# A decoder block on one core: constant products between the chunks of maxima in latent attention, and the next norm's statistics in two parts

## The reference

```
def mla_attention(x, Wq, Wdkv, Wuk, Wuv, Wo, ln_g, ln_b):
    q = (x @ Wq.T).reshape(b, t, 16, 16).transpose(0, 2, 1, 3)
    latent = layernorm(x @ Wdkv.T, ln_g, ln_b)
    k = (latent @ Wuk.T).reshape(b, t, 16, 16).transpose(0, 2, 1, 3)
    v = (latent @ Wuv.T).reshape(b, t, 16, 16).transpose(0, 2, 1, 3)
    q, k = apply_rope(q), apply_rope(k)
    scores = jnp.einsum('bhqd,bhkd->bhqk', q, k) / np.sqrt(16)
    scores = jnp.where(causal, scores, -jnp.inf)
    attn = jax.nn.softmax(scores, axis=-1)
    out = jnp.einsum('bhqk,bhkd->bhqd', attn, v).transpose(0, 2, 1, 3).reshape(b, t, 256)
    return out @ Wo.T
```

## Time and profile before

| | |
|---|---|
| three runs | 2920.39 us median, 2918.30 to 2927.64 |
| the profiled execution | 2920.24 us |
| its span, first to last instruction | 2918.5 us |
| mean granted clock of TensorE | 0.939 |
| TensorE busy | 2728.7 us (93%) |
| VectorE busy | 1394.6 us (48%) |
| ScalarE busy | 1090.1 us (37%) |
| GpSimd busy | 298.3 us (10%) |

### The profile page before, as it was taken

The page is one execution under the profiler, slowest core; times in us unless marked ns, Lnnn a source line. Parts: engine busy times, 40 slices in busy tenths (PEclk is TensorE's granted clock), DMA queues, the critical chain, the costliest instruction groups (busy, mean ns, idle before and its releaser), DMA issues.

```text
span 2918.5 us, 43672 instructions
## 1 busy us (share of the span) xinstructions
PE 2728.7 (93%) x16662; PEld 1708.1 (59%) x16663; DVE 1394.6 (48%) x3906; ACT 1090.1 (37%) x2028; POOL 298.3 (10%) x457
## 2 busy tenths in 40 slices
PE   7999999988999999988999999998999999986998
PEld 4565665454565665454555665455556565456997
DVE  3434466643333456643333456643333457643443
ACT  3444232543444332543443332543453332531221
POOL 1000010122000010122000010122000010023111
PEclk9999996998999996998999996988999997988999
DMA  3000000001000000001000000001000000022111
GB/s 95 11 12 1 15 1 1 2 13 40 12 12 0 15 1 1 2 13 40 11 12 1 15 1 1 1 13 40 12 12 1 15 1 1 2 124 86 54 54 40
DMA packets 32426, 57.09 MB, mean 20 GB/s; under 512 B 6981, under 2 KB 23443, under 8 KB 31859
## 3 DMA queue, kind: packets, MB, share of 16 engines
q1 hardware_dynamic: 27490, 41.56, 4.5%
q0 software_dynamic: 4752, 13.02, 1.2%
HBM read 40.24 MB, written 14.32 MB: 19 GB/s over the span
## 4 chain that ended last, share of the span: by engine, by line
PE 85%; issue 4%; DVE 4%; ACT 3%; POOL 2%; another core or an unknown queue 1%; DMA 0%; DVEq 0%; ACTq 0%; POOLq 0%
PE ps L942 9%; PE ps L1189 8%; PE ps L914 8%; PE ps L1157 8%; PE ps L887 7%; PE ps L1207 6%; PE ps L872 5%; PE ps L932 5%; PE ps L1278 4%; PE ps L1292 4%; PE ps L897 4%; PE ps L1034 3%; PE ps L1052 2%; PE ps L843 1%
## 5 line engine op out<-in xcount | busy, mean ns | idle before, releaser
L1157 PE MATMUL ps<-arena 32*128 32x512 f32 (+3 forms) x1536 | 480.2, 642 | 13.6 <-DVE arena L1552 10.2
L1380 DVE TENSOR_REDUCE neg_max<-ps 128x1 f32<-128x128 f32 (+7 forms) x256 | 194.0, 758 | 608.8 <-PE ps L917 550.8
L780 ACT ACTIVATE arena<-ps 128x1024 f32<-128x1024 f32 (+1 forms) x320 | 300.5, 939 | 453.6 <-PE ps L1189 453.1
L1189 PE MATMUL ps<-arena 32*128 32x256 f32 (+1 forms) x2560 | 400.0, 424 | 0.0
L914 PE MATMUL ps<-arena 128*128 128x512 f32 (+3 forms) x768 | 303.2, 507 | 31.0 <-ACT arena L707 15.6
L942 PE MATMUL ps<-arena 128*128 128x512 f32 (+3 forms) x768 | 319.2, 503 | 5.3 <-ACT arena L698 1.4
L1189 PEld LDWEIGHTS ps<-arena 32*128 32x128 f32 x2560 | 240.2, 205 | 135.4 <-issue 106.9
L698 ACT ACTIVATE arena<-ps 128x512 f32<-128x512 f32 (+3 forms) x384 | 188.1, 491 | 295.9 <-PE ps L932 293.9
L914 PEld LDWEIGHTS ps<-arena 128*128 128x128 f32 x768 | 143.4, 197 | 168.6 <-issue 137.9
L1157 PEld LDWEIGHTS ps<-arena 32*128 32x128 f32 x1536 | 195.9, 218 | 75.3 <-DVE arena L1562 23.7
L887 PE MATMUL ps<-turned_t,arena 128*128 128x512 f32 x512 | 230.6, 604 | 1.1 <-ACT turned_t L669 1.1
(11 more groups left out here) (215 smaller groups left out, 3819.8 us busy)
## 6 DMA issues: line engine op xcount, KB each, us to landing
arena<-in_w_qkv SPq DMA_DIRECT2D x32, 384.0 KB, 3.0
arena<-in_w SPq DMA_DIRECT2D x2, 4096.0 KB, 16.9
xin<-in_x SPq DMA_DIRECT2D x5, 1024.0 KB, 5.6
xres_ids<-sorted_res SPq DMA_DIRECT2D x35, 129.0 KB, 2.2
xin<-sorted_rows SPq DMA_DIRECT2D x35, 128.0 KB
w_out<-in_w_out SPq DMA_DIRECT2D x1, 1024.0 KB
out<-xin,out_row POOLq DMA_INDIRECT x35, 2.7
sorted_res<-xin SPq DMA_DIRECT2D x4, 129.0 KB
```

Source lines behind the costliest of these rows:

```text
L780: nc.scalar.activation(mprobs_t[n % BUFS][:, 2 * pair:2 * pair + 2, 0:QUARTER + more], ps[:, bank:bank + 2, 0:QUARTER + more], ACT.Exp).th ...
L1157: nc.tensor.matmul(ps[:, MAX_BANK[m], 0:n], q_heads_t[rows_j, g, t * P:(t + 1) * P], k_heads_t[rows_j, g, c * BANK:c * BANK + n], start=Tr ...
L1189: last = nc.tensor.matmul(ps[:, 3 + j, kb * QUARTER:kb * QUARTER + n_q], k_heads_t[rows_j, g, keys_at:keys_at + P], q_heads_t[rows_j, g, ( ...
L1380: nc.vector.tensor_reduce(neg_max[:, par, t:t + 1], ps[:, buf:buf + 2, :].rearrange("p a n -> p (a n)")[:, 0:n], AX.X, ALU.max, negate=Tru ...
```

## The change

Three edits. On TensorE the wait for all key copies moves ahead of chunk 6, and behind each of chunks 6 to 53 stands one `keep_warm` product into bank 7. On VectorE the statistics of `xin` are taken in two parts, half 0 behind `take_max` of unit 9, half 1 behind that of unit 10. On GpSimd the scales of half 0 follow the mask of unit 9, those of half 1 the mask of unit 10.

```diff
+NEXT_STATS = (9, 10)
...
-            def self_scales(step, b, use):
-
-                for h in range(2):
+            def self_scales(step, b, use, halves=range(2)):
+
+                for h in halves:
...
                 for u in range(len(UNITS)):
-                    if u == 12:
-                        self_scales(step, b, NORM_NEXT)
                     keep_causal(u)
+                    if u in NEXT_STATS:
+                        self_scales(step, b, NORM_NEXT, [NEXT_STATS.index(u)])
...
                 chunks(0, 6)
                 for use in range(NG, 2 * NG):
                     turn_keys(use)
-                chunks(6, ISSUED)
                 pe.wait_ge(kt_taken, b * (2 * NG) + 2 * NG)
+                for s in range(6, ISSUED):
+                    chunks(s, s + 1)
+                    keep_warm(1, 7)
                 pe.wait_ge(ms_taken, b * MAX_SLOTS + chunk_count(ALONE - 1, TAKE_LEAD) + 1)
...
                             take_max(u)
-                            if u == 13:
+                            if u in NEXT_STATS:
                                 dve.wait_ge(x_in, b * 16 + 32)
-                                for h in range(2):
-                                    row_stats(step, xin, h)
+                                row_stats(step, xin, NEXT_STATS.index(u))
```

## The result

The changed kernel takes 3103.67 us (median of four runs, 3101.98 to 3106.01); the kernel before, in four runs, 2919.35 us (2907.29 to 2927.64). The ratio is 1.0639, with an interval of 1.0604 to 1.0673: slower by 6.4%. The forecast was 3088 us in a range of 3040 to 3140. The profiled execution of after took 3104.95 us with a span of 3103.2, which is 184.7 us more than the span before.

What follows compares the result with a forecast made beforehand. The prediction took VectorE to bound chunks 6 to 53 and TensorE, at half its clock, items 0 to 5. From 2920.24 us, +256.9 (products), -48.7 (clock) and -40.2 (halves) gave 3088 us, range 3040 to 3140.

Steps and rivals of the forecast that it cites:

- A product is two passes of 0.43 us, and two changes of 0.20 us stand around it: Chunks 6 to 53: products cost 41.3 us and 96 tiling changes 19.2 us a batch.
- Rival (a): Chunks 6 to 53: tiling changes overlap, wholly or in their loads; 3011 us, or about 3050 with half; chance 0.11.
- Nothing hides it; TensorE becomes the bound: Chunks 6 to 53: VectorE waits for TensorE, 1.91 us a chunk against 0.52; the stretch becomes 92.7 us.
- Chunk 6 is 0.5 us later for the wait on the key copies: Ahead of chunk 6: waiting for all eight key copies costs 0.5 us more, making 93.2 us four times.
- The clock stays up through stretch and items: Chunks 6 to 53 into items 0 to 5: a dense stream fills TensorE's gaps and keeps 2.4 GHz; -48.7 us.
- (b): Items 0 and 1: the clock falls again and stays down; 3137 us, or 3112 if it recovers midway; chance 0.14.
- (d): Chunks 6 to 53: the change does not hold the clock in the stretch itself; over 3400 us; chance 0.02.
- Items 0 to 5 in 19.1 us each: Items behind the chunks need 19.1 us of full-clock work a batch, for 125.1 us over four: -48.7 us.
- Part 3, -40.2: Statistics and scales in halves, later in the batch: stalls -22.4, clock -20, rest of the halves +2.2 us.
- the clock term: Clock dips around the statistics' and scales' stalls would go: 5.0 us a batch, 20 us in four.
- Nothing elsewhere: All outside chunks 6 to 53, items 0 to 5 and items 6 to 39: change of 0 us.
- Rival (c): Chunks 6 to 53: products fit beside VectorE's work and the stretch stays 29 us; faster, 2831 us; chance 0.02.

Runs made afterwards that it cites:

- grouped: The changed kernel with its 48 products run four in a row behind each fourth chunk, 24 tiling changes a batch for 96: 2939.54 us, ratio 1.0223.
- narrow: The changed kernel with products of 128 columns instead of 512, same count and height: 3181.22 us, ratio 1.0896.
- one_strip: The changed kernel with products on only the first 32 rows of the array, 512 columns as before: 3123.33 us, ratio 1.0862.
- double_change: The changed kernel with each product cut in two halves of 256 columns around a one-row product of 16 columns: 3522.51 us, ratio 1.2250.
- split_only: The kernel before with statistics and scales in halves, without the products: 2889.14 us, ratio 0.9894.
- every_fourth: The changed kernel with one product behind each fourth chunk only, 12 a batch for 48: 2888.85 us, ratio 0.9910.
- fourth_tail: The changed kernel with a product behind each fourth chunk and behind chunks 49 and 53, 14 in all: 2831.37 us, ratio 0.9851.
- the first set: Follow-up kernels run on one chip with the kernel before beside them, which took 2923.67 us there.
- the second and third: Two further sets of follow-up kernels, each on another chip; the kernel before took 2875.22 and 2875.71 us there.
- the third chip: Chip on which the changed kernel was run once more, unedited: 3064.38 us, ratio 1.0647 to the kernel before.

## Why the prediction came out

**Right in direction and size, and in mechanism but for the reason given for the clock.** The forecast of 3088 us is 16 below the median. The steps:

- *A product is two passes of 0.43 us, and two changes of 0.20 us stand around it*. Confirmed: the stretch is 91.77 us for a forecast of 92.7, and solved for the change it gives (91.77 - 31.0 - 41.3 - 1.2)/96 = 0.19 us. The cycle of the projection was the right row to price it by. Rival (a), overlapped changes at 3011 or 3050, is out, and grouped shows that the price stands behind a change and not in each product. The Trainium skill ("TensorEngine Tiling (Array Packing)", Key Properties) says that changing the tiling mode drains the engine; the trace agrees as far as it can show this: in grouped, chunks in different rows start 0.007 us apart, while beside a full-height product each pass starts only after the columns of the one before and 0.09 us more.
- *Nothing hides it; TensorE becomes the bound.* Confirmed by VectorE's waits. The forecast did not see that a chunk alone costs TensorE much less than 31.0/48 us where chunks of different rows can overlap; its sum was right because the products prevent just that.
- *Chunk 6 is 0.5 us later for the wait on the key copies.* Confirmed: 0.49 us more in each batch.
- *The clock stays up through stretch and items.* Confirmed at 1.00 in all four batches; rivals (b) and (d) are out for this kernel. But the reason given, that a dense stream fills the gaps, does not carry: narrow, one_strip and double_change fill the same gaps, and each lost the clock inside the stretch (0.51, 0.51, 0.52). That this product was of a kind that holds it was luck as far as the forecast's reasoning goes, and 0.02 for (d) was too little.
- *Items 0 to 5 in 19.1 us each* was mis-sized: 20.43 us, so -43.3 and not -48.7. The term took 0.73 of the last batch's 26.14 us as full-clock work, as if the half-clock stretches were bound by the array alone and would shrink by half. 1.3 us a batch don't shrink.
- *Part 3, -40.2*, was mis-sized: -32.1. Its stalls went as said (22.4 us), and split_only shows the part alone at -34.5. The error lies in the clock term and the new pieces. I counted 5.0 us a batch for the clock; around the scales' stall the three items 32 to 34 went from 16.09 to 10.76 us, 5.3 where 3.62 + 16.10x0.21 = 7.0 was expected. Of the 1.7 us between them 0.9 were counted twice: the clock was already down while TensorE stood there (3.62x0.25), and the sum took those microseconds once as stall and once as missing clock. The view stands below this list. Around the first stall, where the clock fell only after the wait, items 28 and 29 gave 3.5 us in three batches (4.9 in one) for 1.99 + 7.00x0.23 = 3.6 expected. The halves of the statistics and scales cost 1.3 us a batch for a forecast of 0.54 (items 16, 20 and 22: +0.56, +0.53, +0.26). The "16 scale operations" are 18, 9 for each half; their 9.71 us were right.
- *Nothing elsewhere* was wrong by 6.8 us: +1.6, +1.0, +2.5 and +1.5 in the four batches, +0.2 ahead of them. Half-clock stretches near the gate lie otherwise in the two traces, and the wait at the next batch's start is 8.4 us in one and 11.4 in the other. I did not isolate the cause.

The kernel before, over the scales' stall (TensorE busy 0.01 us, clock 0.75):

```profile
602.93:606.55 3.62, 0.01 (x1) 0.03 (x1) 1.17 (x4) 1.00 (x2) 3.12 (x7) 0.75 0.01 2
```

The misses add up: -3.7 +5.4 +8.1 +6.8 = +16.6 us over the forecast, which is the 16 us of the result.

Rival (c), faster, was right as a possibility that this edit didn't take: the price turned at 0.46 us a chunk, and the edit costs 1.3. With 14 products for 48 the stretch costs 4.4 us more a batch than before, items 0 to 5 give back 12.8 in the first batch, and the kernel, halves included, is 1.5% faster.

## What to carry to other kernels

To hold TensorE's clock in a stretch that another engine paces, try a few full-height products behind groups of row-tiled work, not one behind each piece: each insertion costs the passes, two tiling changes, and the overlap of the tiles that it separates. Run it beside a version without any product: here 12 a batch gained nothing measurable over the halves alone, and 14 little. Price it by a place in the trace where the same two shapes already alternate, and check each variant in the clock row, since smaller products can cost more than large ones. A gain from a dip of the clock can be less than its length times the missing share, and what the engine idles in the dip must be left out of it.

## What the runs showed of the hardware that I had not expected

**The clock did not follow TensorE's recorded busy time.** Four kernels had the stretch 99.9% or more busy in the record: after at 1.00, narrow at 0.51, one_strip at 0.51, double_change at 0.52. grouped, every_fourth and fourth_tail held it at 1.00 in their first batch with TensorE idle for 0.4 to 1.6 us of the stretch. Giving the product 32 rows (one_strip) or 128 columns (narrow), or cutting it in two around a one-row product (double_change), each sufficed to lose it. What exactly is counted these runs don't tell.

**A tiling change is dearer at half clock**, about 0.3 us for 0.19 at full clock. In narrow the product's two passes of 128 columns need 0.43 us at 1.2 GHz (0.108 us at full clock, doubled, twice), and the next chunk starts 0.72 us behind the product:

```profile
500.34 0.80 PE L828 MATMUL ps<-w_out,ident 128*128 128x128 f32 x2
501.06 2.07 PE L1158 MATMUL ps<-arena 32*128 32x512 f32 x2
```

The 0.3 us of double_change agree.

**The same program takes 1.3 to 1.7% longer on one chip than on another** (the kernel before 2919 and 2924 us in the first runs and the first set, 2875 and 2876 in the second and third), and the place can be seen. At the start of batches after the first, TensorE stands with no releaser that the profile shows. The kernel before and after, in the first runs:

```profile
684.91 1.65 PE L914 MATMUL ps<-arena 128*128 128x384 f32 x2 [8.42 <-issue]
```

```profile
732.68 1.65 PE L915 MATMUL ps<-arena 128*128 128x384 f32 x2 [11.36 <-issue]
```

and after on the third chip:

```profile
725.72 0.91 PE L915 MATMUL ps<-arena 128*128 128x384 f32 x2 [0.33 <-ACT arena L708]
```

From the last product of a batch's items to chunk 0 of the next it is 13.0, 12.5 and 14.6 us shorter there, 40 us in all, against 37 us between the two spans of after (3103.2 and 3066.3). Why TensorE stands there on one chip and not on another stays open. The ratio of after to before was the same on both, 1.064 and 1.065.
